# Twelve gathers of a pair, each put behind its own step of the pair before

## The reference, cut to what matters

```
x = x + L0(x)      # per sequence: a 64x64 matrix chosen by an index
x = x + L1(x)      # q,k,v; new k,v written into pages; attention over the last 256 positions; Wo
x = x + L2(x)      # x @ W[id] + b[id], one of 16 matrices of 512x512 per sequence
x = x + L3(x)      # x @ W.T + low-rank adapter chosen by an index

# L1, for each sequence b, with block tables that may name any page:
k_blocks = k_blocks.at[blk, :, off, :].set(k)       # 64 new rows per sequence
k_all = k_blocks[block_tables]                      # all pages of the sequence, by its table
scores = einsum(qg, k_all) * SCALE, masked to 256 positions
o = einsum(softmax(scores), v_all)
```

## Time and profile before

| | |
|---|---|
| median of 3 runs | 1137.64 us (1135.72 to 1139.66) |
| the profiled execution | 1136.99 us, of which the span of the core is 1135.2 us |
| mean granted TensorE clock | 0.968 of full speed |
| PE busy | 1046.9 us (92%), 6418 matmuls |
| DVE, ACT, POOL busy | 657.5 (58%), 539.7 (48%), 540.4 us (48%) |
| DMA moved | 196.16 MB, mean 173 GB/s |

### The profile page before, as it was taken

One profiled execution on the slowest core, in us unless ns is written; L12 is line 12 of the kernel. 1 busy time (PEld: TensorE's weight loads), 2 busy tenths in 40 slices (PEclk: granted clock), 3 DMA queues, 4 the chain that ended last, 5 costly groups with the idle time before them and its releaser, 6 DMA issues.

```text
span 1135.2 us, 23790 instructions
## 1 busy us (share of the span) xinstructions
PE 1046.9 (92%) x6418; PEld 707.0 (62%) x6418; DVE 657.5 (58%) x1919; ACT 539.7 (48%) x1336; POOL 540.4 (48%) x601
## 2 busy tenths in 40 slices
PE   7989999998479899999999999998998999999997
PEld 6767777676245566666665666665566666656655
DVE  6889895767235455555555555554554555555552
ACT  4457775674344344444444444444444444444440
POOL 3555444368545454454544445444544445454400
PEclk9999999999579999999999999999998999999998
DMA  3434443553356766665666666665665566666640
GB/s 130 143 116 149 139 147 114 163 195 124 91 170 195 213 203 191 203 190 182 212 197 198 187 213 184 181 216 178 198 191 170 184 217 184 178 206 193 199 149 19
DMA packets 95337, 196.16 MB, mean 173 GB/s; under 512 B 31346, under 2 KB 40114, under 8 KB 87110
## 3 DMA queue, kind: packets, MB, share of 16 engines
q1 hardware_dynamic: 63942, 149.49, 40.6%
q0 software_dynamic: 30784, 44.16, 13.9%
q10 hardware_dynamic: 576, 2.10, 0.5%
HBM read 195.08 MB, written 33.56 MB: 201 GB/s over the span
## 4 chain that ended last, share of the span: by engine, by line
PE 60%; issue 4%; ACT 4%; another core or an unknown queue 3%; DMA 2%; POOL 1%; DVE 0%; ACTq 0%; POOLq 0%; DVEq 0%
PE bank L93 21%; PE bank L1361 10%; PE bank L1336 8%; PE bank L1323 8%; PE bank L1315 8%; PE bank L1302 4%; ACT KT L1121 2%; ACT PT L1121 2%; PE bank L1292 1%; DMA KVE<-in_pool,idxs_e 1%; DMA KVE<-kv_scratch,idxs_e 1%; DMA KV<-in_pool,idxs 1%; POOL KVE L1037 0%; POOL KVE L1027 0%
## 5 line engine op out<-in xcount | busy, mean ns | idle before, releaser
L1121 ACT ACTIVATE PT<-bank 112x384 f32<-112x384 f32 x256 | 113.8, 489 | 257.7 <-PE bank L1323 188.2
L1199 DVE CUSTOM_DVE_ANT_0 SM<-bank,FM 128x336 f32<-128x336 f32 x256 | 129.8, 507 | 167.4 <-PE bank L1315 138.2
L1037 POOL DMA_INDIRECT KVE<-kv_scratch,idxs_e x96 | 96.3, 1003 | 125.8 <-DMA KVE<-in_pool,idxs_e 100.9
L1037 POOL DMA_INDIRECT KV<-kv_scratch,idxs x96 | 96.2, 1002 | 122.2 <-DMA KV<-in_pool,idxs 102.7
L1130 ACT ACTIVATE PR<-SM,nb 128x336 f32<-128x336 f32 x256 | 145.6, 575 | 1.4 <-issue 0.6
L1027 POOL DMA_INDIRECT KV<-in_pool,idxs x96 | 95.3, 993 | 74.5 <-PE bank L1336 47.8
L1121 ACT ACTIVATE KT<-bank 128x336 f32<-128x336 f32 x128 | 57.6, 450 | 142.3 <-PE bank L1302 135.1
L1361 PE MATMUL bank<-W,XT 128*64 128x512 f32 x512 | 123.7, 604 | 0.7 <-ACT XT L1121 0.7
L1027 POOL DMA_INDIRECT KVE<-in_pool,idxs_e x90 | 89.1, 990 | 73.0 <-PE bank L1336 49.8
L1315 PE MATMUL bank<-KT,QB 64*128 64x336 f32 x512 | 111.1, 511 | 11.2 <-ACT KT L1121 7.4
L93 PE MATMUL bank<-wqh,XTH 128*128 128x512 f32 x256 | 106.0, 414 | 8.6 <-DVE XTL L485 6.1
(11 more groups left out here) (175 smaller groups left out, 2161.0 us busy)
## 6 DMA issues: line engine op xcount, KB each, us to landing
W<-in_w SPq DMA_DIRECT2D x64, 1024.0 KB
FM<-mask SPq DMA_DIRECT2D x64, 168.0 KB
X<-in_x SPq DMA_DIRECT2D x32, 256.0 KB
x_scratch<-X SPq DMA_DIRECT2D x32, 256.0 KB, 2.0
kv_scratch<-KVR SPq DMA_DIRECT2D x32, 256.0 KB
qt_scratch<-QT SPq DMA_DIRECT2D x32, 256.0 KB
QB<-qt_scratch SPq DMA_DIRECT2D x32, 256.0 KB
XB<-x_scratch SPq DMA_DIRECT2D x32, 256.0 KB
```

What stands on the lines that cost most here:

```text
L1037: pool.indirect_dma_start(out=KV[k][:, c, :], out_offset=None, in_=kv_d, in_offset=bass.IndirectOffsetOnAxis(ap=idxs[k][:, NCH + c:NCH + c ...
L1121: return nc.scalar.activation(dst, src, ACT.Copy)
L1199: v.tensor_tensor_reduce(out=SM[u % 2][:, :], in0=bank[u % 2][:, 0:SPAN], in1=FM[k][:, :], scale=1.0, scalar=-3e38, op0=ALU.add, op1=ALU.m ...
```

## The change

A wait is put ahead of eleven of a pair's twelve gathers: the nine that belong to steps 0, 1 and 2, and two of the step before. `apart(step, c)` waits for a count that TensorE reaches in the pair before the one that is gathered. Gather c = 0 of a group goes behind the scores, c = 1 behind the turned probabilities, c = 2 behind the values. held(b) has the step 2b-1 and fresh(b) the step 2b; the very first gather, c = 0 of held(0), keeps only the wait that it had.

```diff
@@ body of the pool block
+                    def apart(step, c):
+
+                        sem_, done = ((s_s, 2 * step + 2), (s_ptp, 2 * step), (s_pv, 2 * step))[c]
+                        wait_all(pool, s_pass_pool, (sem_, 8 * (p - 1) + done))
+
                     def held(b):
                         k = 2 * pr.par + b
 
                         wait_all(pool, s_pass_pool, (s_pv, used(b)), (s_reg[k], at(pr.i, 1, 0)))
                         for c in range(NCH):
+                            if b or c:
+                                apart(2 * b - 1, c)
                             pool.indirect_dma_start(
...
                         wait_all(pool, s_pass_pool, (s_old[k], at(pr.i, 16 * NCH, 16 * NCH - 1)))
                         for c in range(NCH):
+                            apart(2 * b, c)
                             pool.indirect_dma_start(
```

## The result

| | before | changed |
|---|---|---|
| median (range) of the runs beside each other | 1137.16 us (1135.72 to 1139.66, 4 runs) | 1181.70 us (1169.34 to 1185.41, 4 runs) |
| ratio, 95% interval | 1 | 1.0387 (1.0347 to 1.0428) |
| profiled execution, span of the core | 1136.99, 1135.2 us | 1185.41, 1183.6 us |
| mean granted clock | 0.968 | 0.958 |

The sign was wrong and the time lies outside the range (1114 to 1151). In a later comparison (e9) the same two kernels gave 1.0354 (1.0265 to 1.0442). All ratios here are taken from runs in the faster of the chip's two states, so they can differ a little from the quotient of the medians.

What follows compares the result with a forecast made beforehand. TensorE was taken to bound phase B, with only 19.8 us irregular there. 1136.99 us less 16.4 won plus 5.4 paid gave 1126.0; with 0.65 for the median, 1127 us was forecast, range 1114 to 1151.

Steps and rivals of the forecast that it cites:

- The steady pairs, the schedule: Start times of GpSimd's gathers behind scores 0 in an ordinary pair, a gather following its TensorE step by 1.0 to 1.6 us.
- What is won: Waits at values 3 and behind rows of six gathers shrink: 16.4 us gained, bounds 0 and 20.8.
- the 16.4 us: Gain: 6.45 us from three rows of six, 9 from pairs with early fresh(0), 1 from the early pairs.
- One reading behind it: fresh(0) beginning 0.6 us or less behind scores 0 makes values 3 wait 1.56 us instead of 0.51.
- What is paid: Five gathers in a row from 15.8 to 22.0 us, and the keys' copy before scores 3: 0.2 us a pair, 5.4 us.
- The bound of 2.42: Upper bound in us on the new row's cost in a pair, from a KT wait after an early row of six.
- The row of five does what the rows of six did: Rival, 0.20: at KT of the next pair and PT of values 2, 1.1 us a pair, slower, 1152 us.
- The late queries: Rival, 0.11: queries queue behind sequence 0's later expert matrix in SyncE's queue; at 0.8 us a pair, 1143 us.
- A: Theory of the experiments: TensorE's releases reach other engines late while GpSimd issues gathers without a pause.

Runs made afterwards that it cites:

- e9: The changed kernel, unaltered, run again on one chip with the kernel before: 1179.87 us, ratio 1.0354.
- e3: Against the changed kernel, all three gathers of held(0) wait for values 2 of the step before: 1179.32 us, ratio 1.0318.
- e1: Against the changed kernel, new waits only in held(0) and fresh(0), with held(1) and fresh(1) as before: 1189.36 us, ratio 1.0418.
- e6: Against the kernel before, one new wait: the first gather of fresh(0) behind scores 0: 1158.26 us, ratio 1.0119.
- e7: Against the changed kernel, one new wait for each group of three, at its first gather, behind scores: 1160.73 us, ratio 1.0142.
- e10: Against the changed kernel, held(0)'s first gather waits for ScalarE's second copy for values 2, its second has no wait: 1157.65 us, ratio 1.0172.
- e4: Against the changed kernel, the expert matrix of sequence 0 no longer waits for held(1) to land: 1175.69 us, ratio 1.0286.
- e5: Against the changed kernel, held gathers of the second phase are issued but move next to nothing: 1155.03 us in one run.

## Why the prediction was wrong

**The steady pairs, the schedule: right.** Expected were fresh(0) at 2.3 to 3.3 us, held(1)'s last gather at 12.1 to 12.7, fresh(1) from 15.8 to 16.5, held(0)'s first at 19.7 and last at 23.0 to 23.6. In the pair of 705.08 they start at 2.2, 12.1, 16.3, 20.2 and 24.8. Held(0)'s first is 0.5 us late and its last over a microsecond, since values 2 themselves are late. Where each gather would stand could be had from the trace of before.

**What is won: the mechanism right.** Values 3 wait 0.50 us in nearly every pair. Which part of the 16.4 us came can't be separated, since most pairs now carry something larger. One reading behind it was too clean: in the kernel before, fresh(0) begins 0.4 to 0.6 us behind scores 0 also in the pairs from 525.67, 576.23 and 626.02, and values 3 wait 0.50 us there.

**What is paid: the step that failed.** "I take 0.2 us a pair for it": the row from 16.3 costs 1.4 to 2.3 us of waiting at values 2 in 17 of 25 pairs, 33 us together, and TensorE's own work grows by 0.7 us a pair at the lower clock. With all of the 16.4 won, what was paid would be 44.5 + 16.4 = 61 us, not 5.4. The reason given for the low end was the error: "a row of six broke the rhythm at its fourth to sixth gather, and what TensorE needs at 20 to 22 us (copies for values 2, done at 20.0) is out before". Those copies are due at about 19 us, at the start of the row's third gather, with one gather still to come, and they came at 20.8 and 22.4: they were not out before. They are out where the row starts 0.7 us later, as at 857.46, and then the harm falls on the last keys. And the earlier trace rows already held what counts, the end of the row: its last gather starts at 783.0 (780.39 and two more at 1.3), and values 0 at 785.67, 2.7 us behind it. I read from these rows which gather does harm, where they say until when it lasts. The last gather of the new row starts at 20.2, so by this reading values 2 start at 22.9, where they stood at 21.1, 1.8 us later; measured are 23.0 and a wait of 2.01. In these pairs the row was four long and not five, since its fifth gather waits for a turn that GpSimd itself sees late. The bound of 2.42 was sound; the value in it was not.

**The rivals.** "The row of five does what the rows of six did" had the place and the sign, at 0.20, and was priced at the middle, 1.1 us a pair, for 1152 us. At the upper bound it gives 27 x 2.42 = 65, less 16.4 and with 1 for the clock, 1187 us, near to what was measured. Of the clock I had 1 us in all for what is 0.7 us a pair, 17 us in 25 pairs: with these waits some pairs run at a granted clock of 1.00 and others at 0.94, as 705.08 and 731.68 show. The late queries cost next to nothing here. Their rival had the matrix right and left out `XB1`, which held them at 17.3 us already before, so they moved by 0.3 us and not by some 3.5. That they are a real limit shows in e3, where they take 12.2 us.

**What stays open.** The runs show that the lateness goes with rows of gathers: it moved with the row in e1, e6, e7 and e10, and not with the expert matrix (e4), the held rows' data (e5) or the start of fresh(1) (e10). Where a late copy would stand, A could say once the row was known. What a version would take it could not, since the row that formed was often not the one planned: it missed the times of e1, e3, e6 and e7. The runs don't show what carries the lateness from GpSimd to the releases, and whether the fresh rows' data has a part in it. Nor is its onset sharp: in e3 copies to `PT` that start 0.1 to 0.5 us behind a third gather are in time (731.42 is 0.21 behind it), while here the one due at the start of the third gather of 723.99 comes 1.9 us late. A pause inside a row without any other change wasn't tried. And no version beat the kernel before.

## What to carry to other kernels

Look at a row of gathers by its end. In this kernel, on the usual chips, a copy that is due near the end of a row often comes only some 2 us after the row's last gather has started. So plan to have the last gather start 2 us ahead of the need, or the copy out before the row's third. A gather held back to spread the load pushes all that stands behind it, and the landing waits press them together again elsewhere. And where a cost in every pair is bounded between 0 and 2.4 us, its value decides the sign of the whole: work out when the disputed thing ends and when it is needed, before taking a number near one bound.

## What the runs showed of the hardware

- A release of TensorE that was due near the end of a row of gathers reached ScalarE late. Of 325 late copies behind the last gather of a row, 249 began 1.6 to 2.5 us after its start, which is 0.6 to 1.5 us after it had ended. GpSimd's own wait for the same turn was late too (2.09 us idle, 728.36).
- A wait that GpSimd finds met costs nothing: 0.30 us between gathers with it or without (725.28).
- A gather that started inside VectorE's addition `XBB` (0.68 us) with 0.15 us or more of it left lasted 0.86 us and what was left of it, up to 1.46 us, in 48 of 49 cases (856.88: 1.30). The 290 that started ahead of it and shared 0.3 us or more with it lasted 0.98 to 1.02 us.
- Chips differ. The kernel before took 1115 us on one, and 1137 to 1145 in the four other comparisons. On the fast one no copy behind 402 us waited for "remote", in rows of three or of six.
- Over the 25 pairs with these waits the granted clock was 0.97, 1.00 in the pair of 705.08 and 0.94 in the next.
